# Another order table for one step of an eight-image convolution, attention and expert block

## The reference, cut to what matters

```
x = x + conv_attention(channel_norm(x))      # per pixel, over 256 channels, eps 1e-6
t = tokens(x)                                # (1024, 256)
t = t + experts(token_norm(t))               # eps 1e-5
# conv_attention: qkv = 1x1 conv to 768 channels; agg = 5x5 depthwise conv of qkv, then a 1x1 conv in groups of 8;
#   heads of 8 channels over [qkv, agg]: q, k through relu, v with a column of ones;
#   out = q (k^T v), divided by its last column; 1x1 conv from 512 to 256 channels; batch norm
# experts: 11 logits from the mean token, softmax, the best two make weights of 6 experts;
#   out = sum_e weight_e * (gelu(t W1_e + b1_e) W2_e + b2_e), hidden width 341 each
```

## Time and profile before

| | before |
|---|---|
| median of 3 runs | 1596.1 us (1592.65 to 1596.1) |
| the profiled execution | 1595.73 us |
| its span, first to last instruction | 1594.0 us |
| TensorE busy | 1353.0 us, 85% |
| VectorE busy | 1314.2 us, 82% |
| ScalarE busy | 1061.8 us, 67% |
| GpSimd busy | 985.7 us, 62% |
| TensorE's mean granted clock | 0.94 |

### The profile page before, as it was taken

One profiled execution on the slowest core, in us unless ns is written; L12 is line 12 of the kernel. 1 busy time (PEld: TensorE's weight loads), 2 busy tenths in 40 slices (PEclk: granted clock), 3 DMA queues, 4 the chain that ended last, 5 costly groups with the idle time before them and its releaser, 6 DMA issues.

```text
span 1594.0 us, 18712 instructions
## 1 busy us (share of the span) xinstructions
PE 1353.0 (85%) x6844; PEld 787.1 (49%) x6844; DVE 1314.2 (82%) x1305; ACT 1061.8 (67%) x1855; POOL 985.7 (62%) x746
## 2 busy tenths in 40 slices
PE   5613678689997999989997999899998999899998
PEld 3313555354564556545464556455564546445443
DVE  4899979899989989898979989898979999970100
ACT  4433446567767777767677776867777866765676
POOL 3683457475678558666669558666766647445644
PEclk8757679889999999999999999999999999999999
DMA  5200000000001000010001000010001000100000
GB/s 187 80 0 27 0 27 1 0 27 1 14 1 36 31 14 1 1 67 14 1 1 42 25 14 0 1 40 14 1 1 40 14 1 1 40 1 14 13 7 22
DMA packets 14251, 32.75 MB, mean 21 GB/s; under 512 B 2384, under 2 KB 5328, under 8 KB 13904
## 3 DMA queue, kind: packets, MB, share of 16 engines
q1 hardware_dynamic: 14160, 31.56, 5.6%
HBM read 23.17 MB, written 8.39 MB: 20 GB/s over the span
## 4 chain that ended last, share of the span: by engine, by line
PE 46%; DVE 20%; POOL 13%; ACT 13%; issue 6%; DMA 1%; POOLq 0%; SPq 0%; ACTq 0%
PE wbk L489 19%; DVE dacc L1069 17%; PE acc L502 11%; PE wbk L581 4%; POOL dwo L886 3%; PE wbk L540 3%; PE wbk L600 2%; PE wbk L567 2%; PE wbk L555 2%; ACT gh L686 2%; ACT hb L687 2%; POOL sv L839 2%; ACT hb L781 2%; POOL gl L916 2%; POOL nrm L845 1%
## 5 line engine op out<-in xcount | busy, mean ns | idle before, releaser
L1069 DVE SCALAR_TENSOR_TENSOR dacc<-qkvs,dww,dacc 128x930 f32<-128x930 f32 (+4 forms) x954 | 1053.0, 1184 | 0.0
L916 POOL TENSOR_TENSOR gl<-hb,gh 128x512 f16<-128x512 f32 x256 | 300.4, 1180 | 272.1 <-ACT hb L687 270.3
L886 POOL TENSOR_TENSOR dwo<-dwo,tapb 128x992 f32<-128x992 f32 (+1 forms) x104 | 239.8, 2306 | 99.5 <-ACT tapb L661 95.7
L781 ACT ACTIVATE hb<-wbk,b1s 128x512 f32<-128x512 f32 x256 | 173.8, 683 | 92.0 <-PE wbk L489 87.5
L502 PE MATMUL acc<-gh,w2h 128*128 128x512 f16 x512 | 194.5, 380 | 5.2 <-POOL gl L916 4.0
L502 PE MATMUL acc<-gh,w2l 128*128 128x512 f16 x512 | 194.3, 379 | 0.0
L502 PE MATMUL acc<-gl,w2h 128*128 128x512 f16 x512 | 194.3, 379 | 0.0
L686 ACT ACTIVATE gh<-hb,ewg 128x512 f16<-128x512 f32 x256 | 182.5, 713 | 9.5 <-PE acc L502 6.8
L687 ACT ACTIVATE hb<-hb,ewg 128x512 f32<-128x512 f32 x256 | 181.8, 710 | 0.0
L489 PE MATMUL wbk<-th,w1h 128*128 128x512 f16 x512 | 154.9, 384 | 19.9 <-ACT kt L746 17.5
L489 PE MATMUL wbk<-tl,w1h 128*128 128x512 f16 x512 | 153.6, 382 | 0.0
(11 more groups left out here) (146 smaller groups left out, 2275.5 us busy)
## 6 DMA issues: line engine op xcount, KB each, us to landing
xa<-x SPq DMA_DIRECT2D x8, 1024.0 KB, 4.9
yr<-x SPq DMA_DIRECT2D x8, 1024.0 KB, 5.1
out<-yr SPq DMA_DIRECT2D x16, 512.0 KB, 2.8
dwo<-w SPq DMA_DIRECT2D x1, 2048.0 KB, 11.0
yr<-w SPq DMA_DIRECT2D x2, 1024.0 KB, 16.2
dwo<-w_qkv SPq DMA_DIRECT2D x1, 768.0 KB, 4.5
wp<-w_proj SPq DMA_DIRECT2D x1, 512.0 KB, 12.2
pw<-w_pw SPq DMA_DIRECT2D x16, 24.0 KB
```

The source lines that it names most:

```text
L781: last = nc.scalar.activation(hb[:, f % GB, :], b[:], ACT.Gelu, bias=b1s[:, f % FT:f % FT + 1], scale=1.0 / (X_SCALE * W_SCALE))
L886: ins = nc.gpsimd.tensor_tensor(d3[:, oy, ox], d3[:, oy, ox], t3[:, iy, ix], ALU.add)
L916: nc.gpsimd.tensor_tensor(gl[:, f % GB, :], hb[:, f % GB, :], gh[:, f % GB, :], ALU.subtract).then_inc(g_low, 1)
L1069: ins = nc.vector.scalar_tensor_tensor(out=dst[:, oy, ox], in0=i3[:, jy, jx], scalar=dww[:, m, tap:tap + 1], in1=a3[:, oy, ox], op0=ALU.mu ...
```

## The change

PLAN is written anew, OF_LAST and OF_THIS move a little. Nothing is added or removed: the same instructions with the same operands are issued, in another order on each engine.

```diff
 PLAN = """
-G agg.-1.0.0 agg.-1.0.1 agg.-1.1.0 agg.-1.1.1 b att.-1.1.0 att.-1.1.1 S att.-1.1.2 F S S G att.-1.1.3
...
+F S agg.-1.0.0 agg.-1.0.1 agg.-1.1.0 agg.-1.1.1 G att.-1.1.0 att.-1.1.1 att.-1.1.2 G F G S att.-1.1.3 b
...
-            OF_LAST = {19: ("rden", 1, 0), 21: ("rden", 1, 1), 77: ("max",), 80: ("route",)}
-            OF_THIS = {66: ("rden", 0, 0), 69: ("rden", 0, 1)}
+            OF_LAST = {19: ("rden", 1, 0), 21: ("rden", 1, 1), 75: ("max",), 83: ("route",)}
+            OF_THIS = {67: ("rden", 0, 0), 70: ("rden", 0, 1)}
```

More of the change, by code:

```diff
@@ L225 @@
-F G S b F rbc.2.0.0 rbc.2.0.1 F b agg.0.4.0 G S apply.2.0.0 F apply.2.0.1 F F G S S G S agg.0.4.1 S G
-agg.0.5.0 agg.0.5.1 qkv.1.4.0 F G qkv.1.4.1 F S G F G S S qkv.1.5.0 F G F G S F S G F G b kv.0.1.0 F S G
-kv.0.1.1 qkv.1.5.1 b F F S mask.0.1 b G S G S b G b S F F
+F S agg.-1.0.0 agg.-1.0.1 agg.-1.1.0 agg.-1.1.1 G att.-1.1.0 att.-1.1.1 att.-1.1.2 G F G S att.-1.1.3 b
+scale.-1.1.0 att.-1.1.4 S qkv.0.0.0 att.-1.1.5 att.-1.1.6 att.-1.1.7 b scale.-1.1.1 qkv.0.0.1 qkv.0.1.0
+qkv.0.1.1 high.1.0.0 F back.-1.1.0.0 S back.-1.1.0.1 G F b G F S back.-1.1.1.0 S back.-1.1.1.1 F proj.-1.0.0
@@ new lines @@
+tok.0.0 low.1.0.0 high.1.0.1 G proj.-1.0.1 b proj.-1.1.0 tok.0.1 tok.0.2 tok.0.3 tok.0.4 tok.0.5 low.1.0.1 G
+b proj.-1.1.1 tok.0.6 tok.0.7 F squares.-1.1.0 relu_q.0.0 kv.0.0.0 squares.-1.1.1 sums.-1.1 b S kv.0.0.1
+mask.0.0 relu_q.0.1 F stats.-1.1 rnorm.-1.1 G S att.0.0.0 att.0.0.1 b att.0.0.2 rbc.-1.1.0 rbc.-1.1.1
+apply.-1.1.0 F att.0.0.3 apply.-1.1.1 scale.0.0.0 G att.0.0.4 att.0.0.5 att.0.0.6 att.0.0.7 high.-1.1.0
+high.-1.1.1 qkv.1.2.0 scale.0.0.1 qkv.1.2.1 low.-1.1.0 back.0.0.0.0 qkv.1.3.0 S G low.-1.1.1 logits.-1
@@ L228 @@
+back.0.0.0.1 back.0.0.1.0 qkv.1.3.1 back.0.0.1.1 agg.0.2.0 F S G F exp.-1 agg.0.2.1 agg.0.3.0 F
+squares.2.0.0 squares.2.0.1 S sums.2.0 agg.0.3.1 b F S G G S b stats.2.0 rnorm.2.0 F G G F S S F G G S S b
+rbc.2.0.0 F S b G F S F rbc.2.0.1 agg.0.4.0 apply.2.0.0 agg.0.4.1 G F G F S b agg.0.5.0 b agg.0.5.1 S G S G
+F qkv.1.4.0 G apply.2.0.1 F G S kv.0.1.0 F S F F F G F S G S qkv.1.4.1 G qkv.1.5.0 b qkv.1.5.1 G S F F S G b
+F S b G G kv.0.1.1 mask.0.1 S S F b S G b
 """.split()
```

## The result

| | before | after |
|---|---|---|
| median | 1595.42 us (4 runs, 1592.65 to 1596.1) | 1526.82 us (4 runs, 1524.3 to 1528.56) |
| ratio | | 0.9572, 95% interval 0.9554 to 0.959 |
| profiled execution, its span | 1595.73, 1594.0 us | 1524.3, 1522.6 us |

The changed kernel is 4.3% faster. The forecast was 1542 us with a range of 1524 to 1590 us: the sign, the likeliest case and the range held, and the gain came out larger: the span of the profiled execution is 71.4 us shorter, where I had summed 53.6. By the medians the gain is 68.6 us; the profiled execution of the changed kernel happens to be the fastest of its four.

What follows compares the result with a forecast made beforehand. TensorE and VectorE were both near their limit, waiting for each other, with TensorE's order making VectorE's inputs late. Five steps −44.7, first −5.3, seventh −2.4, end −1.2: −53.6 us, giving 1542 us, range 1524 to 1590 us.

Steps and rivals of the forecast that it cites:

- the likeliest case: Most waits of TensorE and VectorE go: 1542 us, own range 1524 to 1557 us; chance 62%.
- The norm scale: TensorE's norm stretch: waits of 4.55 and 1.57 us go, with the slow spreading (1.7 us); scale ready some 4 us early.
- The small gaps: TensorE's remaining waits at exponentials, attention tiles and back, 0.35 to 1.3 us each; 6.4 us of gaps a step in all.
- TensorE paces: Steady step: TensorE's loop takes 168.0 us, above VectorE's 164.4 us, so TensorE sets the step.
- five steps: Images 2 to 6: 5 × 168.0 = 840.0 against 884.7 us, −44.7 us.
- The first step: From 201.6 to 375.4 us: VectorE's waits for exponentials and logits go, one qkv fewer ahead of att.0.1.7; −5.3 us.
- The seventh step and the end: Seventh step bounded by VectorE, its wait of 2.4 us goes; last 168.9 us shorten by about 1.2 us.
- VectorE's floor: VectorE in a steady step: 161.85 us busy, about 0.7 us of short gaps, 1.8 us of waits: 164.4 us.
- B: Gaps reappear at ScalarE's drains behind splits; only the scale's wait and slow clock saved; about 1567 us; chance 13%.
- C: GpSimd's base adds delay VectorE's centre taps, raising VectorE's floor to 171.3 us a step; 1559 us; chance 5%.
- E: Base taps on GpSimd come too late for VectorE's centre taps; a step takes 180 us, 1611 us in all; chance 15%.
- D: Nothing moves: VectorE's waits shift between small tasks, the step stays at 177 us; 1591 to 1601 us; chance 5%.

Runs made afterwards that it cites:

- Experiment 4: Changed kernel with the norm stretch alone partly put back: base taps before stats, both rbc together behind fewer pieces; 1559.47 us, 0.9775 of before.
- experiment 3: Kernel before, old table and numbers, with only two base taps moved from before stats to behind rnorm; 1597.31 us, 1.0014 of before.
- experiment 7: Kernel before, old table, with the two base taps moved from before stats to behind rbc.2.0.1; 1599.43 us, 1.0036 of before.
- experiment 8: Changed kernel with VectorE's reciprocals at taps 22, 25, 67 and 72 in place of 19, 21, 67 and 70; 1525.63 us, 0.9567 of before.
- experiment 9: Changed kernel with VectorE's routing four taps later, tap 87 in place of 83, nothing else; 1533.56 us, 0.9621 of before.
- Experiment 12: Changed kernel with three S (second products) moved into TensorE's three largest remaining gaps; 1527.58 us, 0.9588 of before.
- experiment 10: Old first half of the table joined to the new second half, letters adjusted to equal piece counts at the join; 1747.29 us, 1.0955 of before.

## Why the prediction was right, and what was off

**The norm scale: right, and larger.** The room on GpSimd was there: the scale is ready at 811.78, TensorE comes at 816.04, 4.3 us later, where I had "some 4 us". The waits of 4.55 and 1.57 us and the slow spreading went. Experiment 4 shows what the stretch is worth, at least 4.7 us a step; experiments 3 and 7 show that the early scale alone is worth nothing. That the four more pieces and the quieter place on ScalarE are what it needs besides is read from the waits for banks there, and no experiment takes them away one by one.

**The small gaps: right.** Forecast and measured in step 4: `ffn.2.31` 1.1 and 1.22 us; `att.4.0.4` to `att.4.0.6` 1.3 and 0.98; `back.4.0.0.0` 0.35 and 0.28. At `att.3.1.2` I had 0.5 and 0.27 came, but with 0.78 at `att.3.1.0` ahead of it, which was there before too. In all TensorE is idle 5.8 us of a step (167.0 − 161.17), where I had 6.4 to 6.8.

**TensorE paces: right for the steady step.** Forecast 168.0, measured 167.0 us. With 161.17 us of work (I had 161.2) this is the one number that carries the result. Experiments 8 and 9 bear it out: VectorE's waits and even 5.4 us more of VectorE's work move the steady step by 0.16 us at most. Experiment 12 limits it: at the gap shown there, what spaces TensorE's pieces is ScalarE's order of drains and splits, so that a gap filled is a gap moved.

**What was mis-sized: the ends, which I priced by VectorE's waits.** The sum has the term "five steps: 5 × 168.0 = 840.0 against 884.7: −44.7 us". By TensorE's marks the five steps gave −45.7 us, so the term holds. It failed by the marks I chose: between VectorE's marks the stretch lost 60.1 us, since VectorE's lead over TensorE grew inside it. Before, VectorE began image 7's taps 1.8 us ahead of `agg.6.0.0` (1260.2 and 1262.0), after, 12.1 us ahead (1190.6 and 1202.7). Of the 17.8 us by which the sum fell short (71.4 − 53.6), 1.0 lies in the five steps. By TensorE's marks the rest lies here:
- *Ahead of the first step*, for which the sum has nothing: `agg.0.0.0` starts at 207.1 us in place of 213.2, 6.1 us sooner, though ORDER is the same up to it. So it is in all fourteen kernels, and yet the mark stood anywhere from 207.0 to 214.2 us in their profiled executions. So this is luck and not the change, as far as is known; what moves the mark stays open.
- *The first step*, −5.3 us by "VectorE waits 12.3 us": from `agg.0.0.0` to `agg.1.0.0` it gave −7.5 us (173.7 and 166.2). In experiment 4 it takes 172.8 us, so 6.6 us of it hang on the norm stretch, with a granted clock of 0.91 there and 0.93 in the changed kernel; the term was near, but for another reason.
- *The seventh step and the end*, −3.6 us: measured 12.1. This is the term that was mis-sized most. I had written that VectorE bounds the seventh step by itself. It did, but TensorE was then waiting for it, as the waits of the kernel before between 1262.0 and 1425.2 us show, and with VectorE's new lead these two waits are gone:

```profile
PE wbk L540 <- DVE dwo L1055: 5.2, 1, 5.2
PE wbk L535 <- DVE dwo L1055: 1.1, 1, 1.1
```

That takes most of the 7.7 us by which the seventh step is shorter (163.2 and 155.5). In the last stretch, 4.4 us shorter, TensorE is busy 6.7 us less and idle 2.3 us more, where I had 5.2 and 3.9. That these 12.1 us don't hang on the norm stretch experiment 4 shows, with 155.4 and 164.4 us for the last two stretches as in the changed kernel (155.5 and 164.4).

**VectorE's floor: wrong.** "VectorE's floor is 161.85 us busy, about 0.7 us of short gaps, and 1.8 us of waits: 164.4 us." VectorE was busy only 156.0 to 157.6 us a step. Most of it (8.3 − 3.4 = 4.9 us) is the routing chain out of GpSimd's way. It cost the forecast little, since VectorE does not pace a steady step: experiment 9, with VectorE busy 161.85 us in its second step, lost 6.8 us, most of it at the ends. But the lower end of the range, 1524 us, is five steps at this floor. The measured 1526.8 us lies barely above it, but with steady steps of 167.0 us, and with what is missing there made up by the ends and the start; that the range held on this side is luck in part.

**The rivals.** B (gaps reappear at ScalarE) did not come in the new table, but experiments 3, 7 and 12 are this rival at work. C had the right mechanism with the wrong sign: the change moved VectorE's small work out of GpSimd's way, and the centre taps, which C has slower, took 83.8 us in all in place of 89.1. E was there in small: the wait of 2.26 us at the centre tap came three times, 6.8 us in all, against the 15 us a step from which it would have decided; in experiment 10 the longest was 23.8 us. D is refuted by the result. Of what I said would show the forecast, two things were wrong: the waits for L760 stayed at 7.46 us a step and not under 3, since VectorE is ahead of TensorE and waits somewhere; and by VectorE's marks, which I had used, one step took 157.8 us and not 165 to 171.

## What to carry to other kernels

Where two engines follow each other through a pipeline, cut the profile at the marks of the engine that paces, and look at the first and last steps for themselves; a follower's lead can grow or shrink by ten microseconds, and its waits then price nothing. In a full stretch, ask whether all inputs of the waiting instruction are early, its buffer and the drain of that among them: here, moving one producer only passed the gap on. In a table whose letters mean "the next piece", a change in one half shifts the meaning of the other, so keep the counts at each point equal before comparing halves.

## What the runs showed of the hardware

- VectorE instructions of 11 to 242 elements with both inputs in SBUF were held until GpSimd's instruction beside them ended: 2.21 in place of 0.17 us (L1003) and 2.48 in place of 0.41 (L1007) in experiment 9. So was L999, which reads one SBUF tensor and scalars: 3.53 in place of 0.49 us for its two in the kernel before. The reduction in the same chain (L1010) took 0.41 us in experiment 9 beside a split of GpSimd, and 0.41 us in the changed kernel without one. The Trainium skill, SBUF — State Buffer, Who interferes with whom, says that a VectorE instruction with two SBUF inputs contends with a GpSimd instruction that reads SBUF, and that a reduction never does; the trace agrees.
- After waits of 2.48 us (experiment 4) and 2.95 us (experiment 3) TensorE's next spreading ran at a granted clock of 0.53 and 0.50, the lower of its two levels (1.2 GHz): 3.65 us for sixteen matmuls, 2.08 us for eight. After waits of 1.49 and 2.67 us (experiments 3 and 7) it ran at 1.00, the higher one (2.4 GHz), and eight took 1.16 us, against 1.05 us without a wait. So the wait's length alone does not say whether the clock falls; I did not find what else does.
